# Cross-attention and MX feed-forward on one core: weight quotients moved to GpSimd, both weight units quantised inside one batch

## What is computed

```python
query = einsum('bnc,dc->bnd', ctx, Wq) + bq;  key = einsum('bnc,dc->bnd', ctx, Wk) + bk
attention = softmax(einsum('bnd,bmd->bnm', query, key))
x = x + einsum('bln,bmn->blm', layernorm(x), attention)

def mx_quant(x):                        # blocks of 32
    amax  = max(abs(xb)); shared_exp = floor(log2(amax)); scale = exp2(shared_exp - 6)
    return clip(round(xb / scale), -128, 127) * scale
def mx_linear(x, W, b): return bf16_round(mx_quant(x) @ mx_quant(W).T + b)

v = bf16_round(layernorm(x))
h = mx_linear(bf16_layernorm(v), W1, b1)     # 512 -> 2048
h = mx_linear(bf16_gelu(h), W2, b2)          # 2048 -> 512
x = x + bf16_round(v + h)
```

## Time and profile before

| | |
|---|---|
| median of 3 runs | 289.44 us (287.11 to 290.83) |
| the profiled execution | 287.0 us |
| its span | 285.2 us |
| busy: PE / DVE / ACT / Pool | 229.8 / 252.3 / 169.1 / 81.6 us |
| mean granted TensorE clock | 0.938 of full speed |

### The profile page before, as it was taken

One profiled execution on the slowest core, in us unless ns is written; L12 is line 12 of the kernel. 1 busy time (PEld: TensorE's weight loads), 2 busy tenths in 40 slices (PEclk: granted clock), 3 DMA queues, 4 the chain that ended last, 5 costly groups with the idle time before them and its releaser, 6 DMA issues.

```text
span 285.2 us, 3245 instructions
## 1 busy us (share of the span) xinstructions
PE 229.8 (81%) x937; PEld 99.1 (35%) x946; DVE 252.3 (88%) x369; ACT 169.1 (59%) x287; POOL 81.6 (29%) x104
## 2 busy tenths in 40 slices
PE   7867559987984099707699798999999989999972
PEld 7423214433431043202344243344444434444320
DVE  2489999999987999999979999699999999899940
ACT  2257136468994276856875999855556555665200
POOL 1067200022005300053420501932312333444453
PEclk9997968999999579766999999999999999999999
DMA  4968999999999635687340228355554376744651
GB/s 150 384 240 180 268 230 195 278 260 237 258 133 283 117 74 137 122 153 148 70 92 18 43 53 129 90 129 130 130 128 77 80 163 133 173 90 97 166 126 58
DMA packets 103077, 42.92 MB, mean 150 GB/s; under 512 B 93844, under 2 KB 96152, under 8 KB 102552
## 3 DMA queue, kind: packets, MB, share of 16 engines
q1 hardware_dynamic: 100224, 35.93, 58.0%
q10 hardware_dynamic: 2360, 6.83, 7.4%
q0 software_dynamic: 480, 0.02, 0.1%
HBM read 15.48 MB, written 4.19 MB: 69 GB/s over the span
## 4 chain that ended last, share of the span: by engine, by line
DVE 50%; PE 15%; ACT 13%; issue 8%; POOL 6%; DMA 5%; SPq 1%; POOLq 0%; ACTq 0%; DVEq 0%
DVE amax L751 13%; PE ps L699 6%; DVE w_int L794 5%; PE ps L711 4%; DVE vw L937 3%; DVE hq L942 3%; DVE pf L858 3%; DVE stats L894 3%; PE ps L654 3%; DMA wst<-in_L_ffn_W 3%; DVE wquant L848 3%; DVE phl L918 2%; DVE nmax L904 2%; DVE xhl L930 2%; ACT phl L558 2%
## 5 line engine op out<-in xcount | busy, mean ns | idle before, releaser
L654 PE MATMUL ps<-pT,xT 128*128 128x512 f16 x192 | 50.0, 416 | 13.6 <-DMA pT<-phl 10.4
L699 PE MATMUL ps<-w1T,cxT 128*128 128x512 bf16 x256 | 58.0, 380 | 0.0
L711 PE MATMUL ps<-w2T,xhl 128*128 128x512 bf16 x247 | 56.7, 379 | 1.6 <-issue 1.0
L554 ACT ACTIVATE wst<-ps 128x1024 bf16<-128x1024 f32 x32 | 32.4, 1020 | 25.6 <-PE ps L699 25.6
L751 DVE TENSOR_REDUCE amax<-phl 128x64 f32<-128x2048 bf16 x16 | 36.5, 2280 | 4.3 <-ACT phl L558 4.3
L654 PEld LDWEIGHTS ps<-pT,xT 128*128 128x128 f16 x192 | 20.0, 106 | 47.7 <-issue 31.6
L642 PE MATMUL ps<-qkT 128*128 128x512 f32 x32 | 18.5, 684 | 21.5 <-ACT pf L453 17.4
L419 POOL TENSOR_TENSOR wst<-wst,vs 128x512 bf16<-128x512 bf16 x16 | 18.5, 1158 | 60.4 <-DVE wquant L853 30.8
L711 PEld LDWEIGHTS ps<-w2T,xhl 128*128 128x128 bf16 x256 | 23.7, 98 | 30.8 <-issue 3.6
L699 PEld LDWEIGHTS ps<-w1T,cxT 128*128 128x128 bf16 x256 | 23.7, 98 | 30.1 <-issue 3.6
L558 ACT ACTIVATE phl<-wst 128x2048 bf16<-128x2048 bf16 x16 | 30.6, 1910 | 1.3
(11 more groups left out here) (77 smaller groups left out, 366.1 us busy)
## 6 DMA issues: line engine op xcount, KB each, us to landing
wst<-in_L_ffn_W ACTq DMA_DIRECT2D x6, 1024.0 KB, 5.8
xs<-in_x SPq DMA_DIRECT2D x4, 1024.0 KB, 8.1
out_x<-wst SPq DMA_DIRECT2D x16, 256.0 KB, 2.8
cx<-in_ctx SPq DMA_DIRECT2D x4, 512.0 KB, 5.4
wst<-in_L_ffn_W SPq DMA_DIRECT2D x2, 1024.0 KB, 9.6
xhl<-pf SPq DMA_TRANSPOSE x17, 4.3
xT<-xhl SPq DMA_TRANSPOSE x16, 4.4
pT<-phl SPq DMA_TRANSPOSE x16, 3.5
```

Source lines behind the costliest of these rows:

```text
L554: act.activation(ys[:, k, 1024 * g:1024 * g + 1024], ps_y[:, 2 * g:2 * g + 2, :], ACT.Copy)\
L654: pe.matmul(ps_pv[:, t % 2, :], xT[:, t, NT * a + n, :], pT[:, :, NT * c + n, :], start=(s == 0), stop=False)
L699: last = pe.matmul(ps_y[:, c, :], h1T[:, k, t, :], w1T[:, 4 * c:4 * c + 4, t, :], start=False, stop=(t == KT - 1))
L711: last = pe.matmul(ps_z[:, k, :], h2T[:, k, t, :], w2T[:, t, :], start=False, stop=(t == FT - 1))
```

## The change

- The quotient of a weight unit goes from DVE to Pool (`over_scale`): in place, float32 in wst times the inverse scale, counted by two new semaphores w1_u and w2_u. There are six steps on w_step instead of seven.
- DVE's `w_clip` waits for that semaphore and clips float32 from wst into int16.
- Units of W1 and W2 of batch b are both begun and finished inside `front(b)`: W1's quotient stands beside the maximum of W2, W2's beside the last energy maximum and the statistics of the next batch. `back` keeps only the second layernorm. The statistics (`x_moments`) are spread, and the quantisation of h1 ends behind W2's product.
- ACT issues the loads of both units of the next batch at the end of its batch: W1 behind the clip of W1, W2 behind the clip of W2 and behind the last `x_plus`, ahead of `query_key`. Pool's quotients stand ahead of the factors of the same batch.
- SP's program is not changed.

The diff, `front` cut to the places that are spoken of:

```diff
@@ -22,7 +22,7 @@
 INV16 = 254 << 7
 XSCALE = 2.0 ** 10
 PSCALE = 2.0 ** 15
-W_STEPS = 7
+W_STEPS = 6
 H_STEPS = 7
 
 
@@ -165,6 +165,7 @@
         ve = [sem(f"ve{n}") for n in range(3)]
         rsr = [sem(f"rsr{n}") for n in range(3)]
         nm, off_rdy = sem("nm"), sem("off_rdy")
+        w_u = [sem("w1_u"), sem("w2_u")]
         v_mean, v_mean2, v_ms = sem("v_mean"), sem("v_mean2"), sem("v_ms")
         rx_rdy = sem("rx_rdy")
 
@@ -379,6 +380,13 @@
                 pool.tensor_tensor(rs[:, 2, :, 0], ms[:, :], mean2[:, :], ALU.subtract).then_inc(ve[2], 1)
                 rsqrt(2, b)
 
+            def over_scale(a, u):
+
+                pool.wait_ge(w_step[a], W_STEPS * u + 4)
+                w = blocks(wst[:, a, :])
+                inverse = mxi[:, a, :, 0:1].broadcast_to([P, NB, BLOCK])
+                pool.tensor_tensor(w, w, inverse, ALU.mult).then_inc(w_u[a], 1)
+
             factors_x(0)
             pool.wait_ge(b1_step, 5)
             for c in range(LT):
@@ -391,10 +399,14 @@
             for n in range(3):
                 pool.dma_start(b2row[n:n + 1, :].rearrange("o (j b) -> o j b", b=P),
                                b2p[:, n, :]).then_inc(row_b2, 16)
+            over_scale(W1, 0)
+            over_scale(W2, 0)
             factors_x(1)
 
             def batch(b, x, v):
 
+                over_scale(W1, b + 1)
+                over_scale(W2, b + 1)
                 if x is not None:
                     factors_x(x)
                 if v is not None:
@@ -516,8 +528,6 @@
                         p_high(front, t - 1)
                     if b is not None and t > 1:
                         x_plus(b, t - 2)
-                    if t == 2 and b is not None:
-                        load_w2(front)
                     if v is not None and t > 0:
                         v_sums(v, t - 1)
                     if v is not None and t < LT:
@@ -528,6 +538,8 @@
                     load_w1(front + 1)
                 if b is not None:
                     x_plus(b, LT - 1)
+                if front + 1 < B:
+                    load_w2(front + 1)
                 if qk is not None:
                     query_key(qk, 0)
                     query_key(qk, 1)
@@ -788,19 +800,13 @@
             def w_inverse(a, u):
                 inverse_scale(w_step[a], W_STEPS * u, a)
 
-            def w_over(a, u):
-                dve.wait_ge(w_step[a], W_STEPS * u + 4)
-                inverse = mxi[:, a, :, 0:1].broadcast_to([P, NB, BLOCK])
-                dve.tensor_tensor(blocks(w_int[:, :]), blocks(wst[:, a, :]), inverse, ALU.mult)\
-                   .then_inc(w_step[a], 1)
-
             def w_clip(a, u):
-                dve.wait_ge(w_step[a], W_STEPS * u + 5)
-                dve.tensor_scalar(w_int[:, :], w_int[:, :], QMAX, None, ALU.min).then_inc(w_step[a], 1)
+                dve.wait_ge(w_u[a], u + 1)
+                dve.tensor_scalar(w_int[:, :], wst[:, a, :], QMAX, None, ALU.min).then_inc(w_step[a], 1)
 
             def w_mult(a, u):
                 wait(dve, (w1T_rdy, w2T_rdy)[a], 16 * u)
-                dve.wait_ge(w_step[a], W_STEPS * u + 6)
+                dve.wait_ge(w_step[a], W_STEPS * u + 5)
                 dve.tensor_tensor(pairs(wquant[:, a, :]), pairs(w_int[:, :]), per_block(mxs[:, a, :, :]), ALU.mult)\
                    .then_inc(w_step[a], 1)
 
@@ -887,13 +893,14 @@
                 dve.wait_ge(step, 4)
                 dve.tensor_copy(part[:, 2, :], f[:, 0, :]).then_inc(step, 1)
 
+            def x_moments(b, t):
+                dve.wait_ge(ld_x[b], 16)
+                dve.bn_stats(stats[:, t, :], xs[:, LT * b + t, :]).then_inc(st, 1)
+
             def x_stats(b):
-                if isinstance(b, int):
-                    dve.wait_ge(ld_x[b], 16)
-                for t in range(LT):
-                    dve.bn_stats(stats[:, t, :], xs[:, LT * b + t, :]).then_inc(st, 1)
-                if isinstance(b, int) and b > 0:
+                if b > 0:
                     dve.wait_ge(rx_rdy, b)
+                    dve.wait_ge(xn_rdy, LT * b)
                 for t in range(LT):
                     wait_alone(dve, st, LT * b + (t + 1), dve_gate)
                     dve.bn_aggr(mv[:, t, :], stats[:, t, :]).then_inc(mvr, 1)
@@ -942,87 +949,77 @@
...
+            def front(b, stats_next, h1):
...
+                w_scale(W2, b)
+                w_clip(W1, b)
+                p_low(b, 1)
+                w_mult(W1, b)
+
+                w_inverse(W2, b)
+                negmax(b, 3)
+                if stats_next is not None:
+                    for t in range(1, LT):
+                        x_moments(stats_next, t)
...
+                x_low(b, 3)
+                w_clip(W2, b)
+                p_low(b, 3)
+                w_mult(W2, b)
                 if h1 is not None:
                     h1_over(h1)
...
-            def back(b, w1, w2, tail):
...
+            def back(tail):
+
+                for t in range(LT):
+                    times_w(tail, t)
+                    plus_b(tail, t)
@@ -1034,21 +1031,13 @@
             split3(b1_step, b1f, b1p)
             dve.wait_ge(ld_b2, 16)
             split3(b2_step, b2f, b2p)
-            w_amax(W1, 0)
-            w_power(W1, 0)
-            w_scale(W1, 0)
-            w_inverse(W1, 0)
-            x_stats(0)
-            front(0, None, None, 1, None)
-            back(0, 0, 0, None)
-            front(1, 1, 0, 2, None)
-            back(1, 1, 1, None)
+            front(0, 1, None)
+            front(1, 2, None)
             dve.wait_ge(ld_ln, 32)
-            front(2, 2, 1, 3, None)
-            back(2, 2, 2, 0)
-            for b in range(3, B):
-                front(b, b, b - 1, None, b - 3)
-                back(b, b, b, b - 2)
+            front(2, 3, None)
+            back(0)
+            front(3, None, 0)
+            back(1)
             for part in tail_parts(B - 3)[LT:]:
                 for part_step in part:
                     part_step()
@@ -1078,9 +1067,6 @@
                     h2_over(m, k)
 
 
-            w_over(W2, B - 1)
-            w_clip(W2, B - 1)
-            w_mult(W2, B - 1)
             parts = tail_parts(B - 2)
             for part in parts[:LT]:
                 for part_step in part:
```

More of the change, by code:

```diff
@@ L943, in plus_b @@
                                          ALU.mult, ALU.add).then_inc(h_rdy, 1)
-            def front(b, w1, w2, stats_next, h1):
-                negmax(b, 0)
+            def front(b, stats_next, h1):
+                if b > 0:
+                    negmax(b, 0)
+                w_amax(W1, b)
+                w_power(W1, b)
+                if b == 0:
+                    for t in range(LT):
+                        x_moments(0, t)
+                    x_stats(0)
+                    negmax(b, 0)
                 normalise(b, 0)
-                if w1 is not None:
-                    w_amax(W1, w1)
                 negmax(b, 1)
@@ L957, in front @@
                 recip(b, 0)
-                if w1 is not None:
-                    w_power(W1, w1)
+                w_scale(W1, b)
                 recip_scaled(b, 0)
-                if w1 is not None:
-                    w_scale(W1, w1)
                 x_low(b, 0)
-                if w1 is not None:
-                    w_inverse(W1, w1)
+                w_inverse(W1, b)
+                w_amax(W2, b)
                 if h1 is not None:
                     h1_amax(h1)
+                else:
+                    x_moments(stats_next, 0)
@@ L969, in front @@
                 negmax(b, 2)
+                w_power(W2, b)
                 normalise(b, 2)
                 recip(b, 1)
+                p_low(b, 0)
+                recip_scaled(b, 1)
+                x_low(b, 1)
+                w_scale(W2, b)
[7 more added lines that the diff above has]
+                        x_moments(stats_next, t)
@@ L972, in front @@
                 if h1 is not None:
                     h1_power(h1)
-                recip_scaled(b, 1)
-                p_low(b, 0)
+                recip(b, 2)
+                normalise(b, 3)
                 if h1 is not None:
                     h1_scale(h1)
-                x_low(b, 1)
+                recip_scaled(b, 2)
+                x_low(b, 2)
+                if stats_next is not None:
+                    x_stats(stats_next)
+                recip(b, 3)
+                p_low(b, 2)
@@ L979, in front @@
                 if h1 is not None:
                     h1_inverse(h1)
-                if w2 is not None:
-                    w_over(W2, w2)
-                negmax(b, 3)
-                normalise(b, 3)
-                recip(b, 2)
+                recip_scaled(b, 3)
+                x_low(b, 3)
+                w_clip(W2, b)
+                p_low(b, 3)
+                w_mult(W2, b)
                 if h1 is not None:
                     h1_over(h1)
-                recip_scaled(b, 2)
-                p_low(b, 1)
@@ L1008, in back @@
-            def back(b, w1, w2, tail):
-                w_amax(W2, w2)
```

(15 more changed lines are left out.)

13 lines of the change are left out of this document (removed).

## The result

The changed kernel takes 349.45 us (median of 4 runs, 348.88 to 349.80) against 289.23 us (4 runs, 287.11 to 290.83) for the kernel before on the same chip: ratio 1.211, 95% interval 1.206 to 1.215. The forecast was 332 us, the range 312 to 351. The profiled span grew from 285.2 to 347.8 us, by 62.6.

The account below looks back on a forecast made before the run. The prediction took the attention half to be bound by DVE. Delays of 10.0, 16.7, 12.5 and 5.3 us in batches 0 to 3 summed to 44.5 on 287.0, giving 331.5, said as 332 us; range 312 to 351.

Parts of the forecast that it names:

- The wait that decides: Batches 1 to 3: DVE's product writing wquant of W2 waits 10 us or more for the previous unit's W2 transposition.
- Sync's piece: From the end of a batch's values to the landing of the W2 transposition: 15.7, 13.8 and 11.5 us.
- when do the values end in the new order: Count from S, a batch's first maximum, to the end of its last values product: S + 26.2, in batch 3 27.0.
- Pool's quotient: Each of eight quotients on GpSimd takes 4.3 us, between 4.0 and 4.6; that bound moves the sum by -2.5 or +2.5.
- Pool shuts DVE out except for one-input reductions: Beside a quotient DVE's one-input maxima and sums go on; its scales, normalisations and two-input operations stand still.
- the 13.6 us saved: DVE work saved: eight quotients, 17.6 us, less 4 us for slower clips; already in the counts, spent under the waits.
- Batch 0: First quotient stands behind Pool's small DMAs, then late load and evictions: first maximum of batch 1 at 46.2, +10.0 us.
- The feed-forward half: Not itself changed, +0; DVE's second chain to its first maximum comes 8 us late, not longer than the first.
- TensorE's clock: Bound: TensorE idles longer and may be granted less clock, 0 to +5 us.
- the transposition in time: Rival: W2's transposition is in time, only Pool, load and eviction waits are left: +16.4, or 303 us; 8%.
- The faster case: Rival at each batch's seam: quotients hide under the maxima and only DVE's work counts, 273 us; 3%.
- A doubled quotient: Rival: the repeated operand doubles each Pool quotient to 8.6 us, +34, or 366 us; 9%.

Follow-up runs that it names:

- e3: The changed kernel with the x loads of batches 2 and 3 issued ahead of the first transpositions: 342.56 us.
- e6: The kernel before with only the quotient on Pool and the clip that reads float32, DVE's and Sync's orders kept: 292.89 us, ratio 1.013.
- e7: e5 with batch 0's two quotients ahead of Pool's fifteen small DMAs instead of behind them: 303.50 us.
- e1: The changed kernel with the W2 transposition of the unit before at the head of Sync's list for a batch: 312.49 us.
- e5: The changed kernel with both the edit of e1 and the early x loads of e3: 308.58 us.
- e9: e6 with x loaded early and DVE reordered: normalisations ahead of the quotients, maximum of W1 and next statistics beside them: 297.35 us.
- e10: Control for e9: same order and loads, with the quotient back on DVE right ahead of its clip: 301.11 us.
- e4: The changed kernel with the quotient back on DVE right ahead of the clip, in the new order: 347.80 us.

## Why the prediction was right, and where it fell short

The sign, the mechanism and its place were right; the forecast was 17 us too low, and the measured 349.45 lies 1.5 us inside the upper end of the range. Stage by stage, on the profiled spans:

| stage | predicted | measured |
|---|---|---|
| batch 0, to the first maximum of batch 1 | +10.0 | +8.2 |
| batch 1 | +16.7 | +29.9 |
| batch 2 | +12.5 | +14.9 |
| batch 3, to the first feed-forward product | +5.3 | +6.5 |
| feed-forward half | 0 | +3.1 |
| sum | +44.5 | +62.6 |

- **The wait that decides** stood where it was put, three times, released by what was named: 20.4, 18.8 and 13.9 us. The values of batches 2 and 3 ended at 127.38 and 178.70, S + 25.7 and S + 27.6 (predicted 26.2 and 27.0). Sync's piece took 17.7, 16.8 and 11.6 us (15.7, 13.8 and 11.5): the first two were under-sized by 5.0 in all, which the bound for it (+6) covers.
- **The step that failed** is the count of batch 1, "when do the values end in the new order". It took the statistics of the next x and the amax of W2 as work that is ready. The values ended at 82.88, S + 37.3 instead of 26.2, and two waits of DVE carry the 11 us (queue rows of Sync first):

```profile
41.87 17.12 SPq L243 DMA_TRANSPOSE pT<-phl  x4
59.03 0.58 SPq L224 DMA_DIRECT2D xs<-in_x  x1
...
55.84 2.29 DVE L763 TENSOR_REDUCE amax<-wst 128x64 f32<-128x2048 f32 x1 [4.03 <-DMA wst<-in_L_ffn_W]
65.19 0.69 DVE L898 BATCH_NORM_STATS2 stats<-xs 128x6 f32<-128x512 f32 x1 [7.07 <-DMA xs<-in_x]
```

  The change moved the first of the statistics ahead of the third row maximum; the load of x for them stands behind four transpositions in Sync's list. This is the same kind of fault as the W2 wait, and the prediction looked for only one of the two. Those four took 17.1 us here and 9.7 in the kernel before, and the first values product waits for them until 61.11, S + 15.5, which the prediction did not count either: in e3, without the wait for x, the values still end at S + 34.2. So the 11 us have three late transfers behind them, W2, x and pT; taking x away gives 3 of them.
- **The range held in part by luck.** No term or bound of it was for those 11 us of batch 1. It held because the over-sized quotient and the bounds for clips and clock, which were not used up, made room.
- **Pool's quotient** was over-sized, 4.3 for 3.64 us: with four to eight on the way, 3 to 5 us of the sum too much. The clip was right: 1.2 us taken, 1.22 measured, eight times. The row of the Trainium skill (VectorE: DVE Perf Modes, The perf-mode tier table), 1227 ns, agrees with it. The Trainium skill (GPSIMD Engine Reference, Performance versus the Vector engine) has 4497 ns for a float32 sum of 2048 columns; this product, whose second operand is a bfloat16 factor repeated over 32 columns, took 3640 in all eight, and the measurement decides.
- **Pool shuts DVE out except for one-input reductions**: right, and dearer than priced. L763 beside a quotient keeps 2.28 us; against that the changed kernel has

```profile
166.89 3.64 POOL L388 TENSOR_TENSOR wst<-wst,mxi 128x2048 f32<-128x2048 f32 x1 [6.46 <-DVE mxi L782]
...
167.33 3.25 DVE L771 TENSOR_SCALAR pow<-amax 128x64 uint32<-128x64 uint32 x1
```

  The prediction spent "the 13.6 us saved" under the waits and expected DVE busy near 239 us. It is busy 250.2: 5.2 us went into L925 (one row), 3.3 into the normalisations (L932) and 3.3 into L771. e6 shows that without any wait for w2T the saving is spent on stretched rows as well.
- **Batch 0**: the quotient behind the small DMAs was right (25.76 predicted as 26.5; e7 gets 4 to 5 us back). From the end of W2's clip to the first maximum of batch 1, with the late load and the evictions, it counted 3.3 us; it was 3.9 (41.69 to 45.57), of which DVE stood 2.1.
- **The feed-forward half** was taken as unchanged. Its first product comes 59.5 us later than before, DVE's first maximum in it 62.2 later: DVE's second chain, priced as "not longer than the first", was 2.7 us longer.
- **TensorE's clock** was given 0 to +5 us. It was granted 0.80, 0.74 and 0.79 of full speed in the three batches (0.87, 0.92 and 0.77 before). Behind a stand of 13.3 us the first values product of batch 2 took 4.61 us, the next one 2.75. No run tells what this was worth in all.
- Of the **rivals**, the transposition in time came true when it was made so: e1, 312.5 us against the 303 given for it. The rival left out the x load waits too, but they are at most half of the 9 us between: e5, without them, is at 308.6. The faster case did not come in any placement tried, the best being e6, 4 us slower than the kernel before. A doubled quotient did not occur.

What stays open: how e7's last 15 us over the kernel before are shared between DVE's waits for energies, most of them at the seams (9.7 us, before none), for the weight loads that arrive late (11.1, before 5.5) and for the LN factors (8.5, before 3.4). The last are not due to the quotients ahead of them on Pool: Pool itself stood idle 2.3, 7.2 and 8.6 us for ScalarE just before these factors. Only the first was tried, and moving the products did not help.

## What to carry to other kernels

When an order is rewritten, list for each moved instruction the semaphores it waits for, and find their producers in the queues that were not rewritten: here one line of Sync's list was worth 37 us and one load 7, where the quotients that the change was about are 18.3 us of DVE's work. A step moved from the end of a batch into it also stops covering something: look at what the other engines did beside it. And work given to GpSimd was not free for VectorE here: between e6 and before it brought nothing, and with maxima and statistics laid beside it (e9 against e10) 4 us.

## What the runs showed of the hardware

- GpSimd's two-input operation on 128x2048 float32 with one operand repeated over blocks takes 3.64 us; in e6 three of eight, each begun 0.1 to 0.2 us into a DVE product (L809), took 4.54 to 4.62. DVE operations on 64 and 512 columns that take 0.18 and 0.54 us alone lasted, begun 0.4 us into it, until its end (3.25 and 3.49); maxima (2.28), statistics (0.68) and reciprocals of one column (0.14) kept their times beside it.
- One DVE row was held before the quotient's own row began, in the changed kernel and alike in e1 (5.87 us); it did not occur in e7, where no DMA list stands ahead of the quotient, nor in e4, where no quotient stands behind the list. Why is open:

```profile
24.21 1.54 POOL L400 DMA_DIRECT2D wqk<-h1q  x3
25.76 3.65 POOL L388 TENSOR_TENSOR wst<-wst,mxi 128x2048 f32<-128x2048 f32 x1
...
24.11 5.86 DVE L925 SCALAR_TENSOR_TENSOR phl<-pf,rinv,phl 128x512 f16<-128x512 f32 x1
```

- The issue of DMA transpositions is slower beside loads on another engine's queue: in the changed kernel four pT took Sync 5.4 us in batch 3 with no such load beside them, 8.4 in batch 1 beside 1 MB from ScalarE's queue, and 17.1 in batch 0 beside 2.5 MB; with those 2.5 MB beside them they took 14.5 to 19.6 in the other kernels of this order.
